# The halves of four shared PSUM banks crossed: one half holds attention scores while the other holds row maxima

## What is computed

```
q_ = (q @ Wq.T + bq).reshape(B, Sq, HEADS, D_K).transpose(0, 2, 1, 3)
k_ = (k @ Wk.T + bk).reshape(B, Sk, HEADS, D_K).transpose(0, 2, 1, 3)
v_ = (v @ Wv.T + bv).reshape(B, Sk, HEADS, D_K).transpose(0, 2, 1, 3)
scores = jnp.einsum('bhqd,bhkd->bhqk', q_, k_) / jnp.sqrt(jnp.float32(D_K))
attn = jax.nn.softmax(scores, axis=-1)
ctx = jnp.einsum('bhqk,bhkd->bhqd', attn, v_)
```

## Time and profile before

| | |
|---|---|
| time, median of 3 runs | 386.16 us (385.46 to 386.75) |
| the profiled execution, its own time | 387.89 us |
| its span, first to last instruction | 386.1 us |
| PE busy, share of the span | 363.5 us, 94% |
| VectorE busy | 184.4 us, 48% |
| ScalarE busy | 149.5 us, 39% |
| first attention, iterations -1 to 8 | 15.3 to some 206 us of the span |

### The profile page before, as it was taken

How to read it: one execution, slowest core, us unless ns; L and a number is a source line. 1 busy time by engine, 2 the same in 40 slices (tenths; PEclk the granted TensorE clock), 3 DMA queues, 4 the chain that set the end, 5 groups by cost and what they waited for, 6 DMA issues and landing times.

```text
span 386.1 us, 7928 instructions
## 1 busy us (share of the span) xinstructions
PE 363.5 (94%) x3108; PEld 273.3 (71%) x3108; DVE 184.4 (48%) x565; ACT 149.5 (39%) x361; POOL 57.0 (15%) x95
## 2 busy tenths in 40 slices
PE   3889999999999999999998999999399999999997
PEld 2546665766567566656687998998368879888875
DVE  4864345656574574654362112111558767623500
ACT  0424553644445535434444121120024668514210
POOL 2720000010101010100120000040763420200000
PEclk9999999999999999998999999999659999999999
DMA  8926060604201000000207389950210011021100
GB/s 247 354 82 220 0 220 2 218 15 163 69 3 28 14 14 1 3 13 3 66 18 233 98 317 335 323 170 24 60 37 0 3 49 53 2 75 42 32 23 25
DMA packets 24886, 35.29 MB, mean 91 GB/s; under 512 B 2609, under 2 KB 21409, under 8 KB 24737
## 3 DMA queue, kind: packets, MB, share of 16 engines
q1 hardware_dynamic: 22160, 31.73, 25.8%
q0 software_dynamic: 768, 1.84, 1.6%
q10 hardware_dynamic: 1920, 1.21, 1.1%
HBM read 31.06 MB, written 3.72 MB: 90 GB/s over the span
## 4 chain that ended last, share of the span: by engine, by line
PE 51%; DVE 2%; ACT 1%; issue 1%; POOL 1%; DMA 0%; DVEq 0%; ACTq 0%; POOLq 0%; SPq 0%
PE ps L572 7%; PE ps L716 7%; PE ps L582 7%; PE ps L694 6%; PE ps L474 5%; PE ps L647 3%; PE ps L637 2%; PE ps L663 2%; PE ps L349 2%; PE ps L451 1%; PE ps L428 1%; POOL xn L1324 1%; PE ps L707 1%; PE ps L724 1%; PE ps L640 1%
## 5 line engine op out<-in xcount | busy, mean ns | idle before, releaser
L1049 DVE TENSOR_REDUCE mneg<-ps 112x2 f32<-112x750 f32 x64 | 57.1, 933 | 42.8 <-PE ps L414 42.4
L828 ACT ACTIVATE heads<-ps 125x896 f32<-125x896 f32 x48 | 41.4, 915 | 19.6 <-PE ps L434 19.6
L1263 POOL TENSOR_TENSOR rstd<-veps,neghalf 112x1 f32<-112x1 f32 x32 | 18.3, 573 | 200.6 <-DVE veps L1015 200.4
L414 PE MATMUL ps<-heads 32*112 32x375 f32 x256 | 38.8, 518 | 1.6 <-DVE mneg L1049 1.0
L358 PE MATMUL ps<-ctxT,w_in 128*128 128x375 f32 x64 | 27.0, 547 | 7.4 <-DMA ctxT<-in_ctxT 6.0
L428 PE MATMUL ps<-heads 32*125 32x224 f32 x384 | 33.0, 374 | 0.7 <-DVE mneg L1049 0.3
L572 PEld LDWEIGHTS ps<-xT,ring 128*128 128x128 f32 x256 | 29.8, 192 | 1.2 <-ACT xT L783 0.7
L572 PE MATMUL ps<-xT,ring 128*128 128x112 f32 x256 | 29.9, 275 | 0.5 <-ACT xT L783 0.5
L716 PE MATMUL ps<-heads,ring 128*112 128x256 f32 x128 | 28.8, 382 | 0.0
L582 PE MATMUL ps<-ring,heads 128*112 128x256 f32 x128 | 28.8, 379 | 0.0
L451 PEld LDWEIGHTS ps<-heads,vones 125*17 125x17 f32 x768 | 17.6, 98 | 13.9 <-issue 12.5
(11 more groups left out here) (139 smaller groups left out, 534.1 us busy)
## 6 DMA issues: line engine op xcount, KB each, us to landing
ring<-in_L_ffn_W SPq DMA_DIRECT2D x16, 1024.0 KB, 6.5
ctxT<-in_ctxT SPq DMA_DIRECT2D x8, 375.0 KB, 11.1
heads<-in_L_ffn_W SPq DMA_DIRECT2D x2, 1024.0 KB, 9.9
ring<-x_by_odd_rows_dram SPq DMA_DIRECT2D x4, 448.0 KB, 3.6
ring<-in_mask SPq DMA_DIRECT2D x1, 1312.5 KB, 7.0
expert_in_dram<-eo SPq DMA_DIRECT2D x1, 896.0 KB, 10.8
b2row<-in_L_ffn_b SPq DMA_DIRECT2D x8, 112.0 KB, 7.6
out_dram<-ring SPq DMA_DIRECT2D x8, 112.0 KB, 2.0
```

What stands on the lines that cost most here:

```text
L414: mm = pe.matmul(bank(j)[0:S, 0:S2], qz[rows, m, a, b * S:(b + 1) * S], kt[b % 3][rows, m, :], start=True, stop=True)
L828: act.activation(pT[w % 2][0:KC, pair.start:pair.stop, :], ps[0:KC, pair.start:pair.stop, 0:2 * QW], ACT.Exp, scale=DK ** -0.5).then_inc(f ...
L1049: v.tensor_reduce(mneg[:, b % 2, PAIRS * g + pair.start:PAIRS * g + pair.stop], ps[0:S, pair.start:pair.stop, 0:S2], AX.X, ALU.max, negate ...
```

## The change

Each step of scores is cut into its two halves, and each of the first three groups of maxima too. In slots 0 to 5 one half takes maxima and the other takes scores: slot u fills half `HALVES[u % 2]` with maxima of group u // 2 and the other half with scores of step u // 2. Slot 6 fills both halves with the maxima of group 3. PE issues the maxima of a slot ahead of its scores. The stages in the slots are placed anew: the weighted sums go from slots 1, 3, 5 to 2, 4, 6; K0 goes from slot 3 to 1; V1 and V2 from 2 and 4 to 3 and 5; the two halves of the query projection are split over two iterations (Q0 in slot 4 of even iterations, Q1 in slot 3 of odd ones, where both stood in slot 3 of even ones). The four waits for the last score step name LOW instead of HIGH, as LOW is now filled last. The projections for the second attention move a little. No computation is added or removed: the same matmuls, reductions and exponentials are issued, with the same shapes.

```diff
-SCORE_AT = {0: 0, 2: 1, 4: 2}
-MAX_AT = {1: 0, 3: 1, 5: 2, 6: 3}
-WEIGHTED_AT = {1: 0, 3: 1, 5: 2}
+WEIGHTED_AT = {2: 0, 4: 1, 6: 2}
...
     0: [("NM1", 0), ("C1", 1), ("D5", 2), ("V0", -1)],
-    1: [("C2", 1), ("C6", 2)],
-    2: [("C3", 1), ("V1", -1), ("D6", 2)],
-    3: [("K0", -2)],
-    4: [("L2", 1), ("ND0", -1), ("V2", -1)],
-    5: [("C4", 1), ("NM0", -1)],
+    1: [("C2", 1), ("C6", 2), ("K0", -2)],
+    2: [("C3", 1), ("D6", 2)],
+    3: [("V1", -1)],
+    4: [("L2", 1), ("ND0", -1)],
+    5: [("V2", -1), ("C4", 1), ("NM0", -1)],
     6: [("U", 0), ("C5", 1), ("K1", -2), ("ND1", -1)],
...
-Q_SLOTS = {2: "QX", 3: "QP"}
+Q_SLOTS = {(0, 3): "QX", (0, 4): "Q0", (1, 3): "Q1"}
...
-CTX_FILL = {"C2": 1, "C3": 1, "C4": 4, "C5": 1, "C6": 2}
-CTX_AT = {(6, 1): 1, (6, 3): 1, (7, 0): 1, (7, 4): 2}
+CTX_FILL = {"C2": 1, "C3": 1, "C4": 3, "C5": 1, "C6": 2}
+CTX_AT = {(6, 1): 1, (6, 6): 1, (7, 0): 1, (7, 1): 1, (7, 3): 1, (7, 5): 1}
...
+def score_half(i, u):
+
+    if 0 <= i < NB and u < 2 * SCORE_STEPS:
+        return u // 2, HALVES[1 - u % 2]
+
+
+def max_halves(i, u):
+
+    if i + 1 < NB:
+        return u // 2, HALVES if u == SLOTS - 1 else HALVES[u % 2:u % 2 + 1]
...
-            def scores(b, step):
+            def scores(b, step, half, pair):
 
                 for m, _ in blocks_of(step):
                     read(("NM", b, m))
+                open_tiles(("ST", b, step), half)
                 for x, (m, c) in enumerate(blocks_of(step)):
...
+                    for j in pair:
+                        rows = slice(32 * j, 32 * j + 32)
+                        pe.matmul(bank(j)[0:KC, x * QW:(x + 1) * QW].rearrange("p (a q) -> p a q", a=2),
+                                  kt[b % 3][rows, m, c * KC:(c + 1) * KC], qz[rows, m, :, b * S:(b + 1) * S],
+                                  start=True, stop=False)
+                    for j in pair:
+                        rows = slice(32 * j, 32 * j + 2)
+                        mm = pe.matmul(bank(j)[0:KC, x * QW:(x + 1) * QW], onesc[rows, :], maxT[rows, m, :],
+                                       start=False, stop=True)
+                mm.then_inc(filled[half], 1)
...
             for i, u in steps():
-                if 0 <= i < NB and u in SCORE_AT:
-                    scores(i, SCORE_AT[u])
-                if i + 1 < NB and u in MAX_AT:
-                    row_max(i + 1, MAX_AT[u])
+                if max_halves(i, u):
+                    row_max(i + 1, *max_halves(i, u))
+                if score_half(i, u):
+                    part, (half, pair) = score_half(i, u)
+                    scores(i, part, half, pair)
                 if 0 <= i < NB and u in WEIGHTED_AT:
                     weighted(i, WEIGHTED_AT[u])
```

More of the change, by code:

```diff
@@ L95, in blocks_of @@
     return [divmod(2 * step + x, NKC) for x in range(2)]
+def score_half(i, u):
[4 more added lines that the diff above has]
+        return u // 2, HALVES if u == SLOTS - 1 else HALVES[u % 2:u % 2 + 1]
 def extras(i, u):
+    if (i % 2, u) in Q_SLOTS and i >= 0 and i // 2 + 1 < QCHUNKS:
+        yield Q_SLOTS[i % 2, u], i // 2 + 1
     for stage, behind in PIPE[u]:
@@ L365, in turn_x, with project_q @@
                     transpose_x("XT1", b, next_bank(SPARE))
-            def project_q(c):
+            def project_q(c, ms):
                 for b in (2 * c, 2 * c + 1):
                     read(("XT1", b))
-                for m in range(DT):
+                for m in ms:
                     n = next_bank(SPARE)
@@ L400, in _, with row_max @@
             pe.wait_ge(ld["wq"], 16)
-            project_q(0)
+            project_q(0, range(DT))
             pe.wait_ge(ld["wv"], 16)
-            def row_max(b, g):
+            def row_max(b, g, halves):
                 m, a = divmod(g, 2)
@@ L409, in row_max @@
                 read(("Q", b // 2, m))
-                for half, pair in HALVES:
+                for half, pair in halves:
                     open_tiles(("MX", b, g), half)
@@ L788, in place_k @@
                 if b >= 3:
-                    act.wait_ge(*filled_at(("ST", b - 3, SCORE_STEPS - 1, HIGH)))
+                    act.wait_ge(*filled_at(("ST", b - 3, SCORE_STEPS - 1, LOW)))
                 for m in ms:
@@ L793, in place_k, with place_q @@
                        .then_inc(free, 1)
-            def place_q(c):
-                for m in range(DT):
+            def place_q(c, ms):
+                for m in ms:
                     o, free = full(("Q", c, m))
@@ L819, in _, with exps @@
             act.wait_ge(bq_par_ready, 1)
-            place_q(0)
-            def exps(b, step):
+            place_q(0, range(DT))
+            def exps(b, step, half, pair):
                 w = SCORE_STEPS * b + step
@@ L825, in exps @@
                     act.wait_ge(pv_units, w - 1)
[L826 to L829, removed]
+                _, free = full(("ST", b, step, half))
+                act.activation(pT[w % 2][0:KC, pair.start:pair.stop, :], ps[0:KC, pair.start:pair.stop, 0:2 * QW],
+                               ACT.Exp, scale=DK ** -0.5).then_inc(free, 1)
             def post(stage, b):
@@ L855, in post @@
                     if b:
-                        act.wait_ge(*filled_at(("ST", b - 1, m + 1, HIGH)))
+                        act.wait_ge(*filled_at(("ST", b - 1, m + 1, LOW)))
                     act.activation(maxT[:, m, :], o.bitcast(BF16)[:, 0:QW], ACT.Copy).then_inc(free, 1)
@@ L875, in _ @@
             for i, u in steps():
-                if 0 <= i < NB and u in SCORE_AT:
-                    exps(i, SCORE_AT[u])
+                if score_half(i, u):
+                    part, (half, pair) = score_half(i, u)
+                    exps(i, part, half, pair)
                 for stage, b in extras(i, u):
@@ L1129, in _ @@
             v.wait_ge(ld["b1"], 16)
-            v.wait_ge(*filled_at(("ST", NB - 1, SCORE_STEPS - 1, HIGH)))
+            v.wait_ge(*filled_at(("ST", NB - 1, SCORE_STEPS - 1, LOW)))
             v.tensor_copy(bq_wide[:, :, :], bcol[:, 2, :].unsqueeze(2).broadcast_to([P, DT, S]))\
@@ L1390, in _ @@
             sp.dma_start(wv_at1, kp_of("L1_xattn_Wv")).then_inc(ld_wv_at1, 16)
-            wait_filled(("ST", NB - 1, SCORE_STEPS - 1, HIGH))
+            wait_filled(("ST", NB - 1, SCORE_STEPS - 1, LOW))
             for r, name in enumerate(("L1_xattn_Wq", "L1_xattn_Wk")):
```

27 lines of the change are left out of this document (5 added, 22 removed).

## The result

| | before | after |
|---|---|---|
| time, median of 20 runs each on the same chip | 385.75 us (383.46 to 388.38) | 388.17 us (386.25 to 389.29) |
| ratio after / before, 95% interval | 1 | 1.0053 (1.0035 to 1.0071) |
| the profiled execution, its own time | 387.89 us | 387.27 us |
| its span | 386.1 us | 385.5 us |
| iteration -1's first start to the experts' first matmul | 15.30 to 206.79 | 15.30 to 208.11 |

The changed kernel is slower by 0.53%, 2.0 us (1.4 to 2.7); the two medians stand 2.4 apart. The two profiled executions stand the other way round, and the last two lines of the table say why. In the part that the change touches, the first attention, the changed kernel is 1.32 us longer. The rest, whose code did not change, came out 1.92 us shorter in this one execution.

The account below looks back on a forecast made before the run. PE's queue, 94% busy including hidden bank waits, was the bound. Iterations 2 to 5 +1.5, 6 +0.3, 0 and 1 -1.0 and -0.6, -1 +0.4, 7 +0.3: +0.9, less 0.1, +0.8, from 386.16 to 387.0 us; range 383.4 to 391.5.

Parts of the forecast that it names:

- the stall in slot 4: Iterations 2 to 6: scores wait for VectorE's reduction, 1.21 us in even, 0.88 in odd iterations, 1.69 in iteration 6.
- The rival of a further stretch at half clock: One more stretch at half clock, from PE's waits in slot 4 or half-filled arrays in iteration 7: 388.7 us, chance 0.10.
- P: PE time of a mixed pair of halves, taken as 1.20 us; adds 1.20 us per iteration in 0 to 6.
- The rival with P = 1.29 or 1.57: A pair costs more than 1.20 us: 389.8 us at 1.29, 398 at 1.57; chance 0.20, nearly all near 390.
- The waits that go: PE's waits for banks, removed by the crossing: 1.74 us in even iterations, 2.29 in odd ones.
- The rival (VectorE free at 2.6 after C3): VectorE reaches group 1's HIGH half sooner than 3.8 us: 380.3 us, or 383.6 at half; chance 0.24, mostly near 384.
- Iterations 2 to 5: Waits removed against pairs and stalls added: even +0.67 us, odd +0.08, twice, together +1.5.
- Iterations 0 and 1: Waits of about 2.7 and 2.1 us go, pairs add 1.20 each, 0.5 and 0.3 remain: -1.0 and -0.6.
- Iteration -1: Six half groups of maxima add 2.4 us, idle and hidden waits return 2.5, two new waits of some 0.45: +0.4.
- Iteration 6: Pairs 1.20, stall 1.69 and a further wait 0.29, less 2.88 us of old waits and idle: +0.3.
- Iteration 7: Six score halves add 3.5 us; against it idle 1.50 and 1.7 for the old half-clock stretch: +0.3.
- its fringe: 0.1 us taken off the +0.9 sum for the pair's fringe in slots where a wait covers it.

Follow-up runs that it names:

- Experiment 4: Changed kernel with slot 2's weighted sum issued between that slot's maxima and scores, so each half runs alone: 396.47 us, ratio 1.0226 to the kernel before.
- Experiment 1: Changed kernel with the router's D6 operations moved from slot 2 to slot 3, behind the reduction PE waits for: 384.82 us, ratio 0.9931 to the kernel before.
- Experiment 6: Changed kernel with D6 in slot 3, iteration 7's score steps whole, and Q1 moved to slot 2 of odd iterations: 380.72 us, ratio 0.9856 to before.
- Experiment 2: Control: the kernel before, uncrossed, with the router's D6 operations moved from slot 2 to slot 3: 386.27 us, ratio 0.9979.
- experiment 5: Changed kernel with iteration 7's score steps whole, in slots 0, 2, 4: 385.39 us, ratio 0.9990; with D6 also in slot 3: 381.33 us, 0.9896.

## Why the prediction was right, point by point

The changed kernel is slower, as forecast, and 388.17 lies within 383.4 to 391.5. That range is 8 us wide, so the number alone says little. The two terms on which the argument rests, the price of a pair and the stall in slot 4, came out as worked out. The sum did not: +0.8 was forecast, and +2.0 measured. It went wrong in iterations 0, 1 and 7, by 1.6 together, and misses the other way in iterations -1 and 6 took 0.5 of that off again, which is luck. The rival of a further stretch at half clock, priced at 388.7, is the nearest number, but it is not what happened: the granted clock is 1.00 in every window up to 208.11.

**The pair of halves: right.** P was put at 1.20, and the pairs at 112.25 and 118.32 (and 115.20) take 1.18. Experiment 4 shows what stands behind it: a half alone costs as much as the whole, and a mixed pair as much as its longer member. The rival with P = 1.29 or 1.57 is excluded; a pair whose scores start behind its maxima takes that much longer (in slot 5 of iteration 1 they start 0.12 behind, and the pair takes 1.29, 60.51 to 61.80). The rule behind P = 1.57, from the Trainium skill (TensorE: Matmul & The Clock Gate, The mechanism), that matmuls begin strictly in program order, does not hold here either: the scores' first passes began at 112.27, and the maxima's second passes, which are earlier in the program, at 112.66.

**The waits that go: right.** Of the 1.74 in an even iteration no wait is left outside slot 4: the pairs of the other slots start together and take 1.18. What comes in small is that a group ahead of a pair takes about 0.1 longer than ahead of other work: C3 1.04 (117.28 to 118.32) and not 0.95, the half projection of the queries 0.95 (124.18 to 125.13) and not 0.81.

**The stall in slot 4: right in place, cause and size.** Forecast 1.21 in even iterations, measured 1.21 (120.91 to 122.12); the reduction was to begin 3.8 after C3 and began 3.75. Experiment 1 took it away and got 1.12 to 1.18 back in iterations 2, 4 and 6. The rival (VectorE free at 2.6 after C3) was right that the kernel would then be faster than before: with 2.36 it is, by 0.7%. But it priced that at 6.7 us below 387.0, and experiment 1 found 4.0 below the changed kernel, as the losses of the odd iterations mostly stayed. As the change was made, VectorE was not free before 3.75.

**Iterations 2 to 5: right, term by term.** The even ones went from 21.76 and 21.77 to 21.66 and 21.68, the odd ones from 20.35 and 20.36 to 21.17 twice. In that is Q1, whose 0.81 moved from the even ones into the odd ones, "nothing in sum". Without it the even ones lose 0.71 (forecast +0.67) and the odd ones nothing (forecast +0.08). Together +1.44, where the forecast was +1.5.

One thing lay under the stall in odd iterations that counts when it goes. The timeline of all engines in iteration 3, from V1 in slot 3 on:

```profile
99.19 1.03 PE L394 MATMUL ps<-w_in,ctxT 128*125 128x256 f32 x4
99.39 0.96 ACT L809 ACTIVATE heads<-ps,bq_par,parity 128x224 f32<-128x224 f32 x2
100.46 0.89 PE L426 MATMUL ps<-heads 32*112 32x375 f32 x4 [0.24 <-issue]
100.95 0.65 PE L438 MATMUL ps<-heads 32*125 32x224 f32 x4
102.11 0.97 PE L459 MATMUL ps<-heads,vones 125*17 125x112 f32 x32
103.34 0.57 PE L426 MATMUL ps<-heads 32*112 32x375 f32 x2 [0.26 <-ACT heads L836]
```

The maxima start 1.27 behind V1 instead of 0.97: 0.30 in which they wait for Q1's copy on ScalarE (99.39, two of them, 0.96 busy). Then 0.49 is left of the stall ahead of the scores, where 0.88 was forecast for both together. So the copy lies under the stall there, as forecast, and costs nothing of its own. With the stall gone (experiment 1) it does: in that run it ends at 101.50, and the maxima start at 101.60. Experiment 6 got 0.16 and 0.28 back in the two odd iterations, not 0.30 each, since the drain of slot 3's scores is the next wait. Behind the weighted sum 0.33 is lost, where 0.29 was forecast.

**Iterations 0 and 1: mis-sized.** This is the step that failed by most. Forecast -1.0 and -0.6, measured -1.21 and +0.69. Again 0.81 is Q1, which iteration 0 gave to 1: without it -0.40 and -0.12. So the term promised 1.6 and gave 0.5. Its first half was right: read from start to start, the waits of before are 2.71 in iteration 0 and 2.06 in iteration 1, against "about 2.7" and "about 2.1". What was too small is what is left of them, 0.5 and 0.3 in the forecast. In iteration 0 it is 0.95: the pairs of slots 0, 1 and 3 take 1.37, 1.46 and 1.29, the values between them 0.10 and the weighted sum ahead of slot 3 0.27 too long. In iteration 1 it is 0.87, all from slot 3's V1 on: there is no D6 in iteration 1, so no stall for Q1's copy to lie under, and the maxima of slot 4 wait (0.32, 56.72 to 57.99), as do those of slot 5 (0.33, 59.28 to 60.51), and both pairs take 1.29. The rest is small: the pairs cost 0.1 less than 1.20, and groups ahead of a pair take some 0.1 longer.

**Iteration -1: one term too large.** Forecast +0.4; -0.40 in its window and some 0.5 ahead of it, +0.1. The two waits of some 0.45 are both there: the first for the queries' copy just ahead of 15.30, and the last in slot 6, whose maxima take 1.21 (24.29 to 25.50) and not 0.83. PE's 11.59 busy of 11.65 does not speak against them, as a wait under the other half counts as busy. What was too large is "six half groups at 0.81, 2.4 us more"; it came to 1.6. The halves of groups 1 and 2 stand in neighbouring slots with nothing on PE between them. Those of group 1 ran side by side, in 0.83 (the row at 19.45, to 20.28); only group 0's were apart, 0.81 and 0.82. Group 2's took 1.66 (21.47 to 23.13), since HIGH waited for a reduction.

**Iteration 6: nearly as forecast.** It was +0.3 and measured +0.09. Its stall came out at 1.65, where 1.69 was forecast: from V1 to the scores 2.61 pass (161.94 to 164.55), 0.27 of wait ahead of the maxima and 1.38 ahead of the scores.

**Iteration 7: the slow stretch mis-sized.** Forecast +0.3, measured +0.78, 0.5 more. It credited 1.7 us for the stretch at granted clock 0.50. Experiment 2's kernel has the same order in iteration 7 up to step 1's scores and had no such stretch there: 5.18 us (173.57 to 178.75), against 6.34 before the change (172.15 to 178.49). So the stretch cost 1.16, as 0.4 of it lay over a wait for ScalarE that is there anyway. The halves cost the 3.5 of the forecast: experiment 5 gets 2.62 back, and 0.92 more turns into idle time (1.10 against 0.18). No stretch at half clock came in the changed kernel, as assumed.

**The total.** Iteration by iteration the traces give +0.1, -0.40, -0.12, +1.44, +0.09, +0.78 and -0.07 for the tail: +1.8, where the forecast had +0.9 before its fringe. The timed runs say +2.0 (1.4 to 2.7), so the part that the change touches accounts for them within their interval. Two things about the half clock remain. The stretch of before in iteration 7 need not be in every execution, and where it is missing the kernel before is up to 1.2 faster; no run here shows how often it is there. And the later stretches are no longer on average than before: 19 of the 20 timed runs of the changed kernel have a mean granted clock of 0.982, as its profiled execution with 13.65 us at half clock, while the 42 runs of the kernel before that stand beside the experiments have 0.973 to 0.986, mean 0.981.

## What to carry to other kernels

A buffer handed back and forth between two engines can be crossed so that both always have something to drain, but halving it is free only where the other half's work fills the array at the same time: here a half alone cost as much as a whole (0.82 and 1.17 us), a mixed pair 1.18, and where there was nothing to pair it with, whole steps were 2.6 us better. After the crossing, look at what the draining engine has queued ahead of the drain that is now waited for; one edit that moved a router's small VectorE operations behind it was worth 4 us, more than the change had cost. Read such waits from start to start: PE's busy share was 94% with them and without. A move of buffers and the places of the other work belong together: each alone made this kernel slower by 1.6% and 2.3%.

## What the runs showed of the hardware

The last part of the kernel, the same code in all versions, takes 176.8 to 179.3 us, and what differs is a stretch at granted clock 0.50 (1.2 GHz) around the gather of the experts' rows, where PE idles and then runs again (after, it idles 5.6 us ahead of 277.72, and the clock falls at 273.1). After, with the columns of the earlier trace rows:

```profile
208.11:385.50 177.39, 166.43 (x1034) 142.74 (x1034) 69.85 (x232) 54.68 (x161) 32.14 (x48) 0.96 0.32 100
273.12:286.77 13.65, 7.97 (x29) 6.08 (x30) 8.67 (x27) 1.36 (x5) 11.56 (x15) 0.50 0.23 63
```

And before:

```profile
206.79:386.10 179.31, 168.65 (x1034) 144.15 (x1034) 69.83 (x232) 54.65 (x161) 32.09 (x48) 0.95 0.31 99
273.41:290.48 17.07, 12.66 (x42) 9.17 (x43) 10.65 (x32) 2.94 (x11) 11.79 (x16) 0.50 0.17 48
```

Eight more profiled executions had 10.2 us of it (three of them, rest 176.8 to 176.9) or 13.7 us (the other five, rest 177.0 to 177.7). From the experts' first matmul on the two traces keep step within 0.02 us until the stretch of after ends; by the time that of before has ended too, they are 1.96 apart, and stay so. That accounts for why the profiled span of the slower kernel is the shorter one, and for why distances in the trace, which repeat within 0.02 us from iteration to iteration, tell such a change sooner than whole times, which scatter by 2 us around their median.
